# Attention kernel: two key tiles to one exponential of 1024 columns, and scores by query in two single banks

## What is computed

```python
logits = jnp.einsum('bhqd,bhkd->bhqk', q, k) / math.sqrt(HEAD_DIM)   # HEAD_DIM = 16, 16 heads
attn = jax.nn.softmax(logits, axis=-1)                               # over 512 keys
vals = jnp.einsum('bhqk,bhkd->bhqd', attn, v)
```

## Time and profile before

| | |
|---|---|
| median of 3 runs | 1313.53 us (1313.08 to 1314.04) |
| the profiled execution | 1318.47 us |
| its span, first to last instruction | 1316.7 us |
| mean granted clock of TensorE | 0.963 of full speed |
| busy over the span | PE 89%, DVE 63%, ACT 38%, POOL 31% |

### The profile page before, as it was taken

The page is one execution under the profiler, slowest core; times in us unless marked ns, Lnnn a source line. Parts: engine busy times, 40 slices in busy tenths (PEclk is TensorE's granted clock), DMA queues, the critical chain, the costliest instruction groups (busy, mean ns, idle before and its releaser), DMA issues. The chain is left out here.

```text
span 1316.7 us, 20913 instructions
## 1 busy us (share of the span) xinstructions
PE 1177.7 (89%) x5606; PEld 696.7 (53%) x5607; DVE 834.3 (63%) x1458; ACT 498.8 (38%) x867; POOL 405.6 (31%) x520
## 2 busy tenths in 40 slices
PE   6996999999999999767999999983799999999997
PEld 3651222222222222344666556652688888888885
DVE  4998777777778776166778877776333333333432
ACT  2430777777777777412221122224112212212211
POOL 1021431111010111022433334426444544544543
PEclk9996999999999999888999999997799999999999
DMA  8885233323332321004331244310133333333332
GB/s 281 305 278 174 66 96 87 97 85 98 95 89 89 105 79 60 33 0 128 97 96 31 65 96 96 80 33 21 29 53 52 48 53 51 48 54 50 49 52 36
DMA packets 108674, 113.04 MB, mean 86 GB/s; under 512 B 26080, under 2 KB 97904, under 8 KB 107600
## 3 DMA queue, kind: packets, MB, share of 16 engines
q1 hardware_dynamic: 90528, 89.05, 23.3%
q0 software_dynamic: 18112, 23.57, 10.2%
HBM read 68.81 MB, written 43.62 MB: 85 GB/s over the span
## 5 line engine op out<-in xcount | busy, mean ns | idle before, releaser
L567 DVE TENSOR_REDUCE neg_max<-by_query 128x2 f32<-128x1024 f32 x256 | 304.3, 1221 | 87.7 <-PE by_query L472 87.6
L619 ACT ACTIVATE k_wu_e<-by_key 128x512 f32<-128x512 f32 x512 | 277.9, 595 | 81.0 <-PE by_key L480 79.9
L480 PE MATMUL by_key<-k_wg_e 99*128 99x512 bf16 x512 | 196.1, 386 | 4.6 <-ACT k_wu_e L619 2.6
L472 PE MATMUL by_query<-k_wg_e 96*128 96x512 bf16 x512 | 180.3, 397 | 11.2 <-PEq L103 7.5
L1330 POOL DMA_INDIRECT out_rows<-y,slot x72 | 113.2, 1572 | 181.8 <-DVE y L1467 176.5
L1423 ACT ACTIVATE gate<-ps_up 128x512 f32<-128x512 f32 x72 | 43.0, 597 | 303.5 <-PE ps_up L69 303.5
L480 PEld LDWEIGHTS by_key<-k_wg_e 99*128 99x128 bf16 x512 | 49.1, 97 | 179.9 <-ACT k_wu_e L619 140.2
L1383 PE MATMUL ps_y<-k_wd_e,acts_T 128*128 x576 | 136.1, 379 | 0.8 <-ACT acts_T L1432 0.8
L492 PE MATMUL pv<-k_wu_e,k_wd_e 128*32 128x512 f32 x1024 | 136.0, 604 | 0.0
L1383 PEld LDWEIGHTS ps_y<-k_wd_e,acts_T 128*128 128x128 f32 x576 | 109.1, 190 | 18.6 <-issue 1.0
L381 POOL CAST k_max_parts<-neg_max 128x16 bf16<-128x16 f32 x32 | 6.1, 190 | 308.2 <-DVE neg_max L567 308.2
(11 more groups left out here) (211 smaller groups left out, 1899.9 us busy)
## 6 DMA issues: line engine op xcount, KB each, us to landing
k_wg_e<-kept_qk SPq DMA_DIRECT2D x384, 64.0 KB, 2.2
kept_qk<-qk_parts SPq DMA_DIRECT2D x32, 384.0 KB, 3.4
kept_v<-v_ones SPq DMA_DIRECT2D x8, 1024.0 KB, 5.8
k_wd_e<-kept_v SPq DMA_DIRECT2D x32, 256.0 KB, 3.0
k_wu_e<-in_xT POOLq DMA_DIRECT2D x8, 512.0 KB, 4.5
kept_heads<-k_wd_e SPq DMA_DIRECT2D x8, 512.0 KB, 2.8
k_heads_in<-kept_heads SPq DMA_DIRECT2D x8, 512.0 KB, 3.9
k_wg_e<-in_wg_e SPq DMA_DIRECT2D x8, 512.0 KB
```

The source lines that it names most:

```text
L472: pe.matmul(by_query[:, k % 4, :], q_rows[0:KROWS, g, h, t * P:(t + 1) * P], k_rows[0:KROWS, g, h, :], start=True, stop=True).then_inc(que ...
L480: pe.matmul(by_key[:, j % 2, :], k_rows[0:SROWS, g, h, kt * P:(kt + 1) * P], q_rows[0:SROWS, g, h, :], start=True, stop=True).then_inc(key ...
L567: dve.tensor_reduce(neg_max[:, g % 2, 2 * n:2 * n + 2], by_query[:, 2 * (n % 2):2 * (n % 2) + 2, :], AX.X, ALU.max, negate=True).then_inc( ...
L619: act.activation(probs[:, key_tile(j) // 2 * G + j // 2 % G, j % 2, :], by_key[:, j % 2, :], ACT.Exp, scale=float(HD) ** -0.5).then_inc(ex ...
```

## The change

The eight banks are dealt out anew. `by_key` gets four: two scores by key fill two neighbouring banks, one exponential reads both (1024 columns), and there are two such pairs. `by_query` gets two single banks, and each score by query has a reduction of its own (512 columns, one maximum). PE waits before every score by query until the reduction of the score two before it has ended, where it waited once for two scores; before a score by key it waits once for two.

The order on PE changes with it. `QUERIES` is now (1, 0, 1, 1), the third score by query of four stands after the fourth score by key, and the fourth after the step of `add_pv`. `turn_max` moves from behind j = 1 to behind j = 3, `turn_heads` from j = 9 to j = 11, both ahead of that j's scores by query. On DVE `normalise` stands after the tenth of 16 reductions, where it stood after the sixth of 8. On ACT `copy_max` and `copy_pv` stand after the second and the fourth pair.

```diff
-        by_query = pb("by_query", [P, 4, S], FP32)
-        by_key = pb("by_key", [P, 2, S], FP32)
+        by_query = pb("by_query", [P, 2, S], FP32)
+        by_key = pb("by_key", [P, 2, 2, S], FP32)
...
-                pool.wait_ge(max_taken, G * TT // 2 * (u + 1))
+                pool.wait_ge(max_taken, G * TT * (u + 1))
...
-        QUERIES = (1, 2, 1, 0)
+        QUERIES = (1, 0, 1, 1)
...
-                pairs = (NG * b + g) * (G * TT // 2) + k // 2
-                if k % 2 == 0 and not (isinstance(pairs, int) and pairs < 2):
-                    pe.wait_ge(max_taken, pairs - 1)
-                pe.matmul(by_query[:, k % 4, :],
+                n = (NG * b + g) * G * TT + k
+                if not (isinstance(n, int) and n < 2):
+                    pe.wait_ge(max_taken, n - 1)
+                pe.matmul(by_query[:, k % 2, :],
...
-                pe.wait_ge(exp_done[j % 2], G * TT // 2 * (NG * b + g) + j // 2)
-                pe.matmul(by_key[:, j % 2, :], k_rows[0:SROWS, g, h, kt * P:(kt + 1) * P],
+                if j % 2 == 0:
+                    pe.wait_ge(exp_done[j // 2 % 2], G * TT // 4 * (NG * b + g) + j // 4)
+                pe.matmul(by_key[:, j // 2 % 2, j % 2, :], k_rows[0:SROWS, g, h, kt * P:(kt + 1) * P],
...
-                        pe.wait_ge(exp_done[buf], G * TT // 2 * u + G + 2 * kt)
+                        pe.wait_ge(exp_done[buf], G * TT // 4 * u + 2 + kt)
...
                     score_by_key(b, g, j)
+                    if j == 3 and next_max:
+                        turn_max(b1, g1)
+                    if j == 11 and prev:
+                        turn_heads(bp, gp, next_max)
                     for _ in range(QUERIES[j % 4]):
                         if ahead:
                             score_by_query(b2, g2, k)
                         k += 1
-                    if j == 1 and next_max:
-                        turn_max(b1, g1)
-                    if j == 9 and prev:
-                        turn_heads(bp, gp, next_max)
                     if j in LATE_PV and prev:
                         add_pv(bp, gp, LATE_PV[j])
                     if j in EARLY_PV:
                         add_pv(b, g, EARLY_PV[j])
+                    if j % 4 == 3:
+                        if ahead:
+                            score_by_query(b2, g2, k)
+                        k += 1
...
-                dve.wait_ge(query_scored, u * G * TT + 2 * n + 2)
-                dve.tensor_reduce(neg_max[:, g % 2, 2 * n:2 * n + 2], by_query[:, 2 * (n % 2):2 * (n % 2) + 2, :], AX.X,
+                dve.wait_ge(query_scored, u * G * TT + n + 1)
+                dve.tensor_reduce(neg_max[:, g % 2, n:n + 1], by_query[:, n % 2, :], AX.X,
                                   ALU.max, negate=True).then_inc(max_taken, 1)
...
-                    if n == 5 and prev:
+                    if n == 9 and prev:
                         normalise(*before(b, g))
...
-            def exponentials(b, g, j):
+            def exponentials(b, g, pair):
 
-                act.wait_ge(key_scored, G * TT * (NG * b + g) + j + 1)
-                act.activation(probs[:, key_tile(j) // 2 * G + j // 2 % G, j % 2, :], by_key[:, j % 2, :], ACT.Exp,
-                               scale=float(HD) ** -0.5).then_inc(exp_done[j % 2], 1)
+                act.wait_ge(key_scored, G * TT * (NG * b + g) + 2 * pair + 2)
+                act.activation(probs[:, key_tile(2 * pair) // 2 * G + pair % G, :, :], by_key[:, pair % 2, :, :], ACT.Exp,
+                               scale=float(HD) ** -0.5).then_inc(exp_done[pair % 2], 1)
```

More of the change, by code:

```diff
@@ L587, in unit @@
                 prev = not (isinstance(b, int) and b == 0 and g == 0)
-                for n in range(G * TT // 2):
+                for n in range(G * TT):
                     if ahead:
                         take_max(b2, g2, n)
-                    if n == 5 and prev:
+                    if n == 9 and prev:
                         normalise(*before(b, g))
             for g in range(2):
-                for n in range(G * TT // 2):
+                for n in range(G * TT):
                     take_max(0, g, n)
@@ L628, in unit @@
                 b1, g1 = b + (g + 1) // NG, (g + 1) % NG
-                for j in range(G * TT):
-                    exponentials(b, g, j)
-                    if j == 1 and not (isinstance(b1, int) and b1 > LAST):
+                for pair in range(G * TT // 2):
+                    exponentials(b, g, pair)
+                    if pair == 1 and not (isinstance(b1, int) and b1 > LAST):
                         copy_max(b1, g1)
-                    if j == 7 and not (isinstance(b, int) and b == 0 and g == 0):
+                    if pair == 3 and not (isinstance(b, int) and b == 0 and g == 0):
                         copy_pv(*before(b, g))
```

## The result

The changed kernel takes 1333.03 us (median of 4 runs, 1328.49 to 1334.04) against 1313.3 (1313.02 to 1314.04): a ratio (of the means) of 1.0143, 95% interval 1.0119 to 1.0166. It is slower, by more than the forecast's middle (1326) and inside its range (1316 to 1336). The profiled execution took 1328.49 with a span of 1326.7, so the profile shows 10.0 us more than the one of before.

A forecast was written before the change was run, and what follows sets the result against it. PE was taken to bound the middle units, with DVE and ACT in slack. Middle units +16.8, last two units −5.2 and start +0.8 sum to +12.4 us, taking the median from 1313.5 to 1326, range 1316 to 1336.

The forecast's parts named there:

- PE is the bound: In units 1 to 29 PE's list of instructions sets the unit, 11.87 us of work in 12.85; DVE and ACT have slack.
- The reduction of 512 columns: On DVE, one reduction of 512 columns takes 0.69 us, between 0.61 and 0.75, read from rows of other widths.
- The stalls of the single banks: In middle units PE waits before six scores by query for a reduction, 0.08 to 0.17 us each, 0.66 a unit.
- The stall of the turning stays: PE still stalls 0.90 us in turn_max, against 0.86 before, despite its later place; the chain from the last reduction takes 1.40.
- The size in a unit: A middle unit takes 0.58 us more, 13.4 instead of 12.85; over 29 units +16.8 us.
- small waits: In the kernel before, 0.12 us a unit of PE stall, put down to scores by key waiting for an exponential; they go.
- signs of being wrong: Reductions of 512 under 0.63 us, turn_max's stall shrinking with its later place, or a PE wait costing more than its length.
- ACT's saving is worth nothing in the middle: Exponentials of 1024 columns save ACT 0.75 us a unit, which in units 1 to 29 is only slack.
- The last two units: Four banks by key bring unit 30 from 12.40 to 10.1 us and unit 31 from 11.74 to 8.85, together −5.2.
- The start: At PE's low clock before unit 1, single banks cost 0.3 us, and unit 0 itself 0.5: +0.8 in all.
- Longer stalls: Rival, 14%: weights load late after waits, or queued reductions don't overlap (0.69 apart, not 0.61); unit 13.8, kernel 1337 us.
- Waits hidden: Rival, 9%: with reductions of 0.60 us or less only turn_max stalls; unit 12.85 as before, kernel 1309 us.

The follow-up runs named there:

- Kernel 4: The kernel before, with the turning of the maxima on PE and its copy on ACT moved from behind j = 1 to j = 5: 1287.40 us, ratio 0.9791.
- Kernel 1: The changed kernel with each maximum taken over 256 of the 512 keys, output not the reference's: 1301.38 us, ratio 0.9896.
- Kernel 3: The changed kernel with the turning of the maxima moved behind the first step of pv of the unit: 1306.46 us, ratio 0.9931.
- Kernel 5: The kernel before with maxima turned behind j = 5, and paired scores by key in by_query's idle banks in units 30 and 31 only: 1285.20 us, ratio 0.9773.
- kernels 6 and 7: Unedited repeats on another chip: the changed kernel, 1331.33 us, ratio 1.0119, and the kernel before, 1317.15 us, ratio 1.0009 to its own other runs.
- the second comparison: The changed kernel run once more, on another chip, against the kernel before there: 1331.33 against 1316.41 us, ratio 1.0119.

## Why the prediction was right, point by point

- **PE is the bound.** Right. Kernel 4 takes away PE's stall and the time follows down to PE's own work.
- **The reduction of 512 columns.** 0.69 forecast, 0.684 measured. The page "VectorE: DVE Perf Modes" of the Trainium skill, section on the TRN2 errata, would have had 0.658, and with it a unit of 13.2; the unit is 13.52. The line through three rows of other widths was the better guide.
- **The stalls of the single banks.** Right in kind, place and count: four of 0.07 and two of 0.15 a unit, 0.60 in all, where four of 0.08 and two of 0.17 were forecast, 0.66. Kernel 1 shows them by shortening their cause.
- **The stall of the turning stays.** Right: 0.94 on average (0.98 in the unit shown) against 0.90 forecast. The chain from the last reduction's end to PE is the same in both kernels, 1.40 in some units and 1.48 in others, 1.44 on average; the forecast had read one of the shorter ones. Kernel 3 shows that the stall can go.
- **The size in a unit** was 0.64 instead of 0.58, over 29 units 18.6 us instead of 16.8. The stalls alone grew by 0.58, as forecast, but by terms that made up for each other: the waits for reductions came out 0.06 smaller, and the waits for exponentials that went away had been 0.06 and not 0.12 (the other half of the forecast's "small waits" is there in both kernels). What the sum lacked is the 0.01 that PE loses behind each wait, 0.05 a unit. One of the forecast's signs of being wrong, that a wait costs more than its bare length, is met to that extent.
- **ACT's saving is worth nothing in the middle.** Right: 0.88 us less a unit, and none of it came through.
- **The last two units.** Unit 30 took 10.13, as forecast (10.1). From unit 31's start to its last score by key it is 7.57, 2.85 less than before, as forecast; but the term of −5.2 was mis-sized by 1.0, most of it since I let it end there. From that last score to the end of the attention it takes 6.11 us against 5.23: the last `pv` steps wait for two exponentials of 1024 columns. The attention's end gained 4.2, not 5.2. Kernel 5, in which the same gain was to stand alone, has the same wait at its end.
- **The start.** Forecast +0.8. Unit 1 starts 0.5 later in the first pair of profiles, but the first score had started 0.4 earlier; from the first score to unit 1 it is 0.9 us more there and 0.6 more in kernels 6 and 7.
- **The sum.** The attention ends 18.6 − 4.2 + 0.5 = +14.8 later (at 560.56 instead of 545.74), forecast +12.4. The profiled execution moved by 10.0 only, since the first profile of the kernel before had 5 us more behind the attention, about what it stood above its median (4.9). The median moved by 19.7. Of this the attention explains 14.8; the other 5 are in no trace, the forecast had nothing for them, and in the second comparison they are not there (14.9). So the median of 1333 is in the range, but 5 of the 7 us by which it misses the middle are spread of the runs as far as these runs show, and the forecast had no term that could meet or miss them.
- **The rivals.** "Longer stalls" (1337) had the sign of the error but not its cause: reductions in a queue do overlap, three in 1.93 us are 0.62 apart. Its price doesn't follow either: 0.08 more at each of the two queued stalls gives a unit of 13.6 and some 1331, not 13.8 and 1337. Its other half, that a wait costs PE more than its length because the next weights load late, is at most the 0.01 above; that it is the weights isn't shown. "Waits hidden" is what kernel 1 makes of it, and it came out at 1301, below the 1309 given: its unit is 12.67 and not 12.88, since the turning stalls for 0.77 and not 0.90, and since the waits for exponentials are gone.

What the forecast missed was no step of its own but an opportunity beside it: the stall of 0.86 us a unit stood in its table, and turning the maxima four scores by key later in the kernel before is worth 2.1%.

## What to carry to other kernels

Ask which engine has no slack, and let no buffer that it waits for turn round in just the time of its own work: a bank taken from the busy engine's loop (by query) and given to one with slack (by key) cost 0.64 us in every unit and gave back 2 to 3 in the two units where the loop was different. When two short operations become one long one, look at what waits for its end last, here the final `pv` steps. And before resizing buffers, add up the bound engine's own work from start to start and compare it with its period: the difference, 0.98 us of 12.85, named the change that paid.

## What the runs showed of the hardware

- Two exponentials of 1024 columns take 1.94 us in a row, 0.92 from one to the next, against 2.16 for four of 512.
- Reductions of 256, 512 and 1024 columns took 0.424, 0.684 and 1.221 us: 1.02 to 1.05 ns a column and some 0.155 fixed.
- PE behind a score that has waited: the score by key that follows it starts after 0.226 us, where it follows after 0.219 without a wait; a step of `pv` after 0.320 against 0.309 (means of the changed kernel and of kernel 1 at the same places).
- One kernel's runs spread by 7 to 9 us (1327.2 to 1335.7, 1312.6 to 1320.0), where units 1 to 29 differ by 0.15 us between two profiles of it. In the changed kernel they go with a mean granted clock of 0.960 to 0.965, in kernel 4 they don't.
